# GpSimd in place of VectorE for the unit-order copies of the rows attention stage

## The reference

```python
B, S, E = (2, 512, 256); H = 16; D = 16
Q = (x @ wq + bq).reshape(B * H, S, D)      # a plain reshape: a head is 32 tokens by 16 channel groups
K = (x @ wk + bk).reshape(B * H, S, D)
V = (x @ wv + bv).reshape(B * H, S, D)
attn = softmax(einsum('bqd,bkd->bqk', Q, K) / sqrt(D))
out = einsum('bqk,bkd->bqd', attn, V).reshape(B, S, E) @ wo + bo + x
out = layernorm(out) * gamma + beta
```

## Time and profile before

| what | us |
|---|---|
| median of 3 runs | 2202.84 |
| the 3 runs | 2202.74, 2202.84, 2204.48 |
| the profiled execution, its own time | 2205.26 |
| its span in the trace | 2203.5 |
| PE busy | 1789.3 (81%) |
| PEld busy | 1367.1 (62%) |
| DVE busy | 1114.1 (51%) |
| POOL busy | 644.0 (29%) |
| ACT busy | 574.2 (26%) |

### The profile page before, as it was taken

How to read it: one execution, slowest core, us unless ns; L and a number is a source line. 1 busy time by engine, 2 the same in 40 slices (tenths; PEclk the granted TensorE clock), 3 DMA queues, 4 the chain that set the end, 5 groups by cost and what they waited for, 6 DMA issues and landing times. The chain is left out here.

```text
span 2203.5 us, 37825 instructions
## 1 busy us (share of the span) xinstructions
PE 1789.3 (81%) x13322; PEld 1367.1 (62%) x13322; DVE 1114.1 (51%) x2126; ACT 574.2 (26%) x1017; POOL 644.0 (29%) x719
## 2 busy tenths in 40 slices
PE   5956766499975868544957994999999999999997
PEld 3545644377742545322534652788888888888887
DVE  4845556666646656551268866233333333333334
ACT  2311011245531434311223662211111111111111
POOL 1421102620014201203316001344434444434432
PEclk8978778699987888856978996999999999999999
DMA  3464615444126333222135311310010010011001
GB/s 103 162 173 127 186 43 148 160 123 115 44 65 179 72 69 69 94 83 82 52 101 169 98 44 37 95 37 37 1 38 36 1 38 36 1 38 36 1 1 39
DMA packets 246973, 167.04 MB, mean 76 GB/s; under 512 B 54315, under 2 KB 238988, under 8 KB 245134
## 3 DMA queue, kind: packets, MB, share of 16 engines
q1 hardware_dynamic: 241671, 158.98, 24.3%
q0 software_dynamic: 1872, 4.23, 0.5%
q10 hardware_dynamic: 3264, 1.57, 0.4%
HBM read 115.02 MB, written 50.22 MB: 75 GB/s over the span
## 5 line engine op out<-in xcount | busy, mean ns | idle before, releaser
L88 PE MATMUL psum<-x_split,w_split 128*128 128x512 f32 x2304 | 560.6, 392 | 7.7 <-DVEq L1478 4.7
L88 PEld LDWEIGHTS psum<-x_split,w_split 128*128 128x128 f32 x2304 | 421.9, 189 | 88.8 <-DVEq L1478 5.2
L1527 POOL TENSOR_TENSOR e_hidden_split<-e_hidden,e_hidden_split 128x512 fp32r<-128x512 f32 x192 | 247.2, 1288 | 503.9 <-DVE e_hidden_split L1509 503.9
L1505 DVE TENSOR_TENSOR e_hidden<-psum,e_silu 128x512 f32<-128x512 f32 x192 | 132.8, 692 | 461.9 <-ACT e_silu L1462 461.5
L786 DVE TENSOR_REDUCE a_maxima<-psum 128x2 f32<-128x512 f32 x384 | 257.4, 687 | 157.7 <-PE psum L577 92.4
L1431 PEld LDWEIGHTS psum<-w_split,e_hidden_split 128*128 128x128 f32 x2304 | 301.5, 191 | 16.2 <-POOL e_hidden_split L1527 1.3
L1431 PE MATMUL psum<-w_split,e_hidden_split 128*128 128x256 f32 x2304 | 306.3, 283 | 1.1 <-POOL e_hidden_split L1527 1.1
L757 ACT ACTIVATE a_probs<-psum 128x512 f32<-128x512 f32 x384 | 224.7, 598 | 262.9 <-PE psum L599 171.5
L1462 ACT ACTIVATE e_silu<-psum 128x512 f32<-128x512 f32 x192 | 114.7, 597 | 645.3 <-PE psum L88 645.3
L577 PE MATMUL psum<-s_k_stack,s_q_stack 96*128 96x256 bf16 x512 | 120.5, 291 | 41.9 <-DMA a_rel_stack<-scr_r 29.2
L95 PE MATMUL psum<-RT,p_w_raw 128*128 128x512 f32 x256 | 117.4, 613 | 13.6 <-PEq L64 13.6
(11 more groups left out here) (217 smaller groups left out, 2360.7 us busy)
## 6 DMA issues: line engine op xcount, KB each, us to landing
w_raw<-in_w_ffn SPq DMA_DIRECT2D x10, 1920.0 KB, 7.4
scr_q<-p_parts SPq DMA_DIRECT2D x40, 384.0 KB, 2.7
scr_k<-p_parts SPq DMA_DIRECT2D x40, 384.0 KB, 2.8
a_q_stack<-scr_q SPq DMA_DIRECT2D x96, 128.0 KB, 3.0
s_q_stack<-scr_q SPq DMA_DIRECT2D x96, 128.0 KB, 2.7
s_k_stack<-scr_k SPq DMA_DIRECT2D x96, 128.0 KB, 2.7
a_k_stack<-scr_k SPq DMA_DIRECT2D x84, 128.0 KB, 2.9
scr_r<-r_parts SPq DMA_DIRECT2D x8, 768.0 KB, 3.5
```

What stands on the lines that cost most here:

```text
L88: last = eng.matmul(out, lhs(a, k), rhs(b, k), start=i == 0, stop=i == len(terms) - 1)
L1505: dve.tensor_tensor(GF[:, s], ps[:, 2 * s + 1, :], SL[:, s], ALU.mult).then_inc(S["hidden"], 1)
L1527: pool.tensor_tensor(GS[:, 1, s], GF[:, s], GS[:, 0, s], ALU.subtract).then_inc(S["g_lo"], 1)
```

## The change

GpSimd makes 15 of the 16 copies of the rows stage; DVE keeps `permute(0, 0)` alone. On GpSimd `permute(0, 1)` stands behind the five memsets and ahead of the `copy_v(0, ...)`, both copies of image 1 stand behind those and ahead of the bias additions, and in the loop `permute(b + 1, 0)` and `permute(b + 1, 1)` stand behind `copy_v(b, 1)` and `copy_v(b, 2)`. The wait for `stacked` goes along with each. The last turn of GpSimd's loop is written out, without copies.

```diff
-                        if rows and more and u in (11, 13):
-                            permute(i + 2, u // 13)
...
                 if rows:
                     permute(0, 0)
-                    permute(0, 1)
                 if softmax:
                     for u in range(UNITS):
                         maxima(0, u)
                         if u == 10:
                             split_max(0, 0, first=True)
-                if rows:
-                    permute(1, 0)
-                    permute(1, 1)
                 step(0, first=True)
...
             @block.gpsimd
             def _(pool):
+                def permute(b, j):
+                    pool.wait_ge(S["stacked"], index(b, 16 * n_stack, 16 * n_stack))
+                    words = [t.bitcast(mybir.dt.int32) for t in ((QS, KS)[j][0:STACK, b % RING], QK[:, j])]
+                    pool.tensor_copy(words[0].rearrange("p g (h s) -> p g h s", s=DH // 2),
+                                    words[1].rearrange("p h (g s) -> p g h s", s=DH // 2)).then_inc(S["permuted"], 1)
...
                         pool.memset(KS[STACK:STACK + SHIFT, r], 1.0).then_inc(S["setup"], 1)
                         pool.wait_ge(S["setup"], 3 + r)
+                if rows:
+                    permute(0, 1)
                 for quad in range(4):
                     copy_v(0, quad)
+                if rows:
+                    permute(1, 0)
+                    permute(1, 1)
                 if bo is not None:
                     pool.wait_ge(S["w_loaded"], 32)
...
-                with pool.Fori(1, IMAGES) as b:
+                def next_values(b, more):
                     for quad in range(4):
 
                         pool.wait_ge(S["pv_done"], b * 4 - 3 + quad)
                         copy_v(b, quad)
+                        if rows and more and quad in (1, 2):
+                            permute(b + 1, quad - 1)
+
+                with pool.Fori(1, IMAGES - 1) as b:
+                    next_values(b, True)
+                next_values(IMAGES - 1, False)
```

## The result

The changed kernel takes 2214.65 us (median of 13 runs, 2209.69 to 2219.48); the kernel before, in the 13 runs shown with it, 2206.39 (2202.17 to 2213.46). The ratio is 1.0034, 95% interval 1.002 to 1.0047: slower by 7.5 us, where 11.8 was forecast. (The ratio is not that of the two medians, which differ by 8.3 us; the intervals given here belong to the ratio.) The changed kernel's median lies 0.15 us from the 2214.8 that was forecast, and that is luck: the median before came out 3.6 us higher in these 13 runs than in the three that the forecast was added to. Executions scatter over some 10 us, more than the three runs of before had suggested, so the profiles are compared within the stage.

The account below looks back on a forecast made before the run. SP's queue was taken to bound most steps (28.1 us from unit 8 to unit 8), DVE's copies only the start. 11.6 + 0 + 0 + 2.7 - 2.5 = 11.8 us slower, giving 2214.8; range 2208.5 to 2223.

Parts of the forecast that it names:

- The start (11.6): Stage start: image 0's key copy waits behind three GpSimd memsets, so PE begins 11.6 us later, hidden by nothing.
- The 0.97: Memsets at the start: one took 4.472 us beside DVE's key copy instead of 3.506; without that copy 0.97 comes off.
- The copy on GpSimd (1.94 estimated): One 2048-word copy on GpSimd: 181 ns plus 0.86 ns an element, 1.94 us; 1.2 on DVE.
- the rival at 4.9: GpSimd slow on short runs of 8 words: 4.9 us a copy, about 29 more, 2232; chance 0.08.
- Image 1 (0): Step 0: image 1's copies done at T + 15 from PE's first matmul, before T + 15.6; half a microsecond won, lost again.
- Stalls in steps 1 to 5 (0): First unit of steps 1 to 5: 2.7 us stalls, absorbed by unit 8 waits or step 4's issue stall; adds 0.
- The second rival: GpSimd's copies reach SP late, so its loads start late: 2 us in each of five steps, 2225; chance 0.1.
- Step 6 (2.7 and 1.4 of clock): Start of step 6: stall of 2.7 us in full, no DMA wait following, plus 1.4 from PE's slower clock.
- The clock in the steps (-4): Steps 1, 2, 3, 5: shorter unit 8 stops keep PE's clock higher, shortening the SP loop 1 us a step.
- The rival that ends on the other side: Not slower: PE's higher clock gives everything back, needing 14.3 us; 2203.5; chance 0.05.
- my signs of being wrong: Copy over 3 us, unit 8 stops vanishing, or SP loop shorter than 28.1 by over 2 us a step.
- twice the gain: Low end of the sum's own range: with doubled clock gain the kernel slows by 7 us.

Follow-up runs that it names:

- the last-pair run: Changed kernel with image 0's key copy ahead of GpSimd's memsets and both image 7 copies behind unit 11 of step 5: 2199.13 us, 0.9954 against the kernel before.
- the second profile of the changed kernel: The changed kernel measured once more, nothing altered: ratio 1.0039 against the kernel before, stage 229.8 us.
- the third experiment: Changed kernel with GpSimd's key copy of image 0 moved ahead of its memsets: ratio 0.9977 against the kernel before, stage 215.0 us.
- the first experiment: Changed kernel with all copies of images 0 and 1 back on DVE, steps' copies still on GpSimd: ratio 0.9983 against the kernel before.
- the first comparison: The changed kernel against the kernel before, in the main measurement: ratio 1.0034 (1.002 to 1.0047).
- the start-only run: Kernel before with images 0 and 1 copied as in the changed kernel, steps' copies on DVE: ratio 1.0058 against the kernel before.

## Why the prediction was right, and where it was off

**The start (11.6).** Measured 14.43 - 2.86 = 11.6, to the tenth. With the start alone moved the same shift stands at PE's first matmul; with the key copy first it is 0.2. The 0.97 that I had taken off for DVE's missing copy came back: the three memsets take 10.64.

**The copy on GpSimd (1.94 estimated).** 1.89. The slope of two one-input rows carried over to 8-word runs, and the rival at 4.9 falls. The 4.4 us that I had worked out from the Trainium skill ("GPSIMD Engine Reference", "Elementwise — side-by-side cycle accounting") is not what this copy takes; its word on one-input work is. The same section says that its 2.6 cycles belong to an operation with two inputs, which I had left out.

**Image 1 (0).** PE's first unit of step 0 came 13.9 us after its first matmul (731.09 - 717.15), where I had T + 15 and before had 15.6. The loads landed 10.1 after it rather than 11. Unit 8 was 11.6 late as said, so the gain was lost.

**Stalls in steps 1 to 5 (0).** 2.58 each for my 2.7 (3.31 in step 4), hidden by the wait at unit 8. SP was never held up by the late copies. In the list of SP's waits (us in total, times, longest) GpSimd's copy stands once, at the start:

```profile
SPq L502 <- POOL a_k_stack L872: 13.4, 1, 13.4
```

The second rival falls.

**Step 6 (2.7 and 1.4 of clock).** The stop is 2.58. Its whole price is better read in the last-pair run: 6.4 us less between unit 8 of steps 5 and 6, against a profile in which the clock was low for a time; in the second profile of the changed kernel the interval (23.4) is 3.8 above that run's 19.6. My 4.1 lies beside the latter. Against the kernel before, whose interval of 22.1 holds the slow clock behind its own stop at unit 8 of step 5, it is 5.2 in the first profile and 1.3 in the second.

**The clock in the steps (-4): this is the term that was mis-sized.** I took 1 us a step off, although I had found 2.8 between units 8 and 12 and a cap near 2. Measured, SP's loop loses 1.9 (6.4 to 4.5) where the clock is at its upper level from unit 8 to the placing. In steps 1, 2, 3 and 5 of all eleven profiles, 18 stops at unit 8 were 3.2 to 7.1 us long, and each time the placing came 6.0 to 6.4 us later at a granted clock of 0.50 to 0.71; 24 were under 2 us, and 22 of these have 4.5 or 4.6 us at 1.00. The two others show that it is the clock and not the stop itself that counts: 1.50 us and then 5.95 at 0.71 (the third experiment, step 5), 1.56 us and then 5.15 at 0.68 (the last-pair run, step 3). In between, in the first experiment, 2.13 us gave 6.42 and 2.29 us gave 4.51. So the changed kernel gained 4 x 1.9 = 7.6 in its first profile and 3 x 1.9 = 5.7 in its second.

The whole gain x can be had only as what is left over in 11.6 + 2.7 + 1.4 - x: the times give 8.2 and 7.1, the second profile's stage 7.3, but the first profile's stage 4.2, beside my 4. That it was larger than 4 rests on the times (x is 5.3 to 11.3 by the interval of the first comparison) and on the 1.9 a step. The stretch from unit 8 of step 3 to that of step 4 seems to gain more, 31.3 us to 26.2 and 28.8 in the two profiles, but the 31.3 stands in one profile alone: the start-only run, whose steps are those of before, has 28.9 there. Its long issue stall comes out differently in each profile, and with it the difference. The reason that I gave for caution (the matmuls after the 2.36 us stop in step 0 turned slow a unit later) was sound for one stop and not for the mean.

The sum was therefore 11.8 for a measured 7.5 (second look 8.6), within the range. The rival that ends on the other side had the mechanism that took the difference; as I read it, it could not reach 14 because the gain is capped by PE's own pace (intervals of 24 to 25 us with stops near 1). Of my signs of being wrong two came in part: in step 1 of the first profile the stop at unit 8 vanished, and the loop there took 24.1 us for 28.1, shorter by more than 2. In the second profile it took 26.9, with a stop of 3.18. Two slips in my sums: twice the gain makes 15.7 - 8 = 7.7 and not 7, and 2202.84 + 11.8 is 2214.6 and not 2214.8.

## What to carry to other kernels

Before an operation goes to another engine, look what stands ahead of it in that engine's queue at the one place where somebody waits: here three memsets of 3.5 us that nobody needed yet cost more than all twelve copies in the steps. A stop of TensorE has two prices, its length and the slow clock behind it; where a loop closed by another queue runs through the units behind the stop, the second price counts even though the first is hidden, and two short stops can be cheaper than one long. And a stall of a step is harmless only where a later wait takes it up: the last step, which had none, was worth its own arrangement.

## What the runs showed that I had not expected

Taking stalls away made the kernel slower: 219.7 us for the stage without stops at the first units, 211.4 with the stops of steps 1 to 5 in place (1.0013 against 0.9954).

TensorE's clock stayed at its lower level (1.2 GHz) through work without a stop: in the first profile of the changed kernel from 883.2 to 896.7, 13.5 us of continuous matmuls at a granted clock of 0.50, behind a stop of 2.58 us; behind the equal stop of the second profile the interval's mean was 0.93. What decides this isn't settled here.

GpSimd's copy made DVE's wait: beside it the query copy took 2.57 us in place of 1.22 (the third experiment), which the prediction had no price for. So the two engines meet not only at semaphores, as I wrote at the start. The Trainium skill ("SBUF — State Buffer", "Who interferes with whom") says that the one that issues first holds the shared ports for the whole instruction; the 2.57 us agree with it, and so do the memset of 1.60 us in place of 0.53 and the three memsets of 10.64 in place of 11.60.
